# Tile loads issued one step ahead, and one slot's x and scale moved from GpSimd and ScalarE to VectorE, in the last stage of a Mamba and mixture-of-experts kernel

## Time and profile before

| | us |
|---|---|
| median of 3 runs | 1452.68 (1452.41 to 1453.63) |
| the profiled execution | 1451.61 |
| its span | 1449.9 |
| busy in it: PE | 1234.7 (85%) |
| DVE | 1030.2 (71%) |
| ACT | 929.2 (64%) |
| POOL | 849.5 (59%) |

### The profile page before, as it was taken

The page is one execution under the profiler, slowest core; times in us unless marked ns, Lnnn a source line. Parts: engine busy times, 40 slices in busy tenths (PEclk is TensorE's granted clock), DMA queues, the critical chain, the costliest instruction groups (busy, mean ns, idle before and its releaser), DMA issues. The chain is left out here.

```text
span 1449.9 us, 27240 instructions
## 1 busy us (share of the span) xinstructions
PE 1234.7 (85%) x8578; PEld 1076.1 (74%) x8578; DVE 1030.2 (71%) x3112; ACT 929.2 (64%) x2106; POOL 849.5 (59%) x1023
## 2 busy tenths in 40 slices
PE   2899999999999999999999999639999899898850
PEld 2777777778777777777877777529989898898850
DVE  4788889989989989998998998534433434443763
ACT  2777877887787787788778778434434444443443
POOL 0365566556656656655665665516666766662577
PEclk9899999999999999999999999859999999999975
DMA  5500010011011001000101000165677667664455
GB/s 167 178 8 23 26 41 31 24 33 38 24 32 38 24 24 40 31 24 33 38 24 31 32 18 17 50 181 153 172 170 164 163 167 179 155 157 107 160 168 167
DMA packets 112934, 119.90 MB, mean 83 GB/s; under 512 B 19888, under 2 KB 99056, under 8 KB 112880
## 3 DMA queue, kind: packets, MB, share of 16 engines
q1 hardware_dynamic: 97744, 94.58, 20.7%
q0 software_dynamic: 14336, 23.08, 8.3%
q10 hardware_dynamic: 800, 1.57, 0.3%
HBM read 70.63 MB, written 48.56 MB: 82 GB/s over the span
## 5 line engine op out<-in xcount | busy, mean ns | idle before, releaser
L1025 POOL TENSOR_TENSOR mamba_arena<-mamba_arena 128x512 f32<-128x512 f32 (+2 forms) x384 | 383.4, 1009 | 299.2 <-DVE mamba_arena L804 201.8
L454 PE MATMUL bank<-identity,mamba_arena 128*128 128x128 f32 x704 | 112.6, 280 | 52.8 <-DVE mamba_arena L913 27.4
L804 DVE TENSOR_TENSOR mamba_arena<-bank,mamba_arena 128x512 f32<-128x512 f32 (+1 forms) x224 | 136.4, 610 | 13.3 <-PE bank L498 7.6
L454 PEld LDWEIGHTS bank<-identity,mamba_arena 128*128 128x128 f32 x704 | 85.1, 146 | 79.9 <-issue 27.3
L1370 PE MATMUL bank<-xt_hi,wsgu_hi 128*128 128x256 f32 x384 | 116.3, 303 | 26.8 <-DVE xt_lo L1753 13.8
L1370 PE MATMUL bank<-xt_lo,wsgu_hi 128*128 128x256 f32 x384 | 111.9, 291 | 0.0
L1370 PE MATMUL bank<-xt_hi,wsgu_lo 128*128 128x256 f32 x384 | 111.8, 291 | 0.0
L662 ACT ACTIVATE mamba_arena<-bank 128x512 f32<-128x512 f32 x192 | 100.2, 539 | 9.0 <-PE bank L454 6.4
L1370 PEld LDWEIGHTS bank<-xt_hi,wsgu_hi 128*128 128x128 f32 x384 | 77.0, 201 | 28.7 <-DVE xt_lo L1753 15.0
L804 DVE TENSOR_TENSOR mamba_arena<-mamba_arena 128x512 f32<-128x512 f32 (+1 forms) x128 | 54.7, 427 | 48.9 <-ACT mamba_arena L662 46.7
L666 ACT ACTIVATE mamba_arena<-x_all,mamba_arena 128x256 f32 (+1 forms) x128 | 69.9, 595 | 20.8 <-DVE mamba_arena L850 15.5
(11 more groups left out here) (365 smaller groups left out, 4475.8 us busy)
## 6 DMA issues: line engine op xcount, KB each, us to landing
experts_arena<-in_egu SPq DMA_DIRECT2D x64, 256.0 KB, 3.4
routed_sum<-zeros SPq DMA_DIRECT2D x1, 8320.0 KB, 27.0
x_all<-in_x SPq DMA_DIRECT2D x32, 256.0 KB, 2.7
token_table<-mamba_arena SPq DMA_DIRECT2D x64, 128.0 KB, 1.7
normed_transposed<-mamba_arena SPq DMA_DIRECT2D x32, 256.0 KB, 2.0
experts_arena<-normed_transposed SPq DMA_DIRECT2D x32, 256.0 KB, 3.4
experts_arena<-in_edown SPq DMA_DIRECT2D x64, 128.0 KB, 3.0
experts_arena<-routed_sum SPq DMA_DIRECT2D x32, 256.0 KB, 3.1
```

Of the source, the lines that this page charges most:

```text
L454: return nc.tensor.transpose(out, in_, identity[:, :])
L804: return nc.vector.tensor_tensor(out, a, b, op)
L1025: return nc.gpsimd.tensor_tensor(out, a, b, op)
```

## The change

Two edits.

SP issues tiles 1 to 4 (not 1 to 3) before its wait for the last routed addition. In turn n it issues tile n + 5 (not n + 4), and no longer at the head of the turn: behind the loads of slots 1 and 3 and before the load of slot 0. The wait ahead of each load still asks that the tile two before it has been split.

Slot 2 was scaled and shifted by ACT (`f_sum * scale + shift`) and added to x by POOL. Now DVE computes `x = f_sum * scale + x` with one scalar_tensor_tensor for each sequence, right behind the shifts of its turn, and ACT adds the shift to x in place with the same two activations as before in number, size and place, now without a scale. ACT waits for DVE's two instructions. POOL's addition of slot 2 (128x512) is gone, and with it POOL's wait.

```diff
@@ SP
-                for t in range(1, LEAD + 1):
+                for t in range(1, LEAD + 2):
                     eng.wait_ge(m_xt_split, t + 7)
                     load_tile(t)
                 eng.wait_ge(added11, 256)
...
                 for n in range(9):
                     if n < 7:
-                        if n + LEAD + 1 < 8:
-                            eng.wait_ge(m_xt_split, n + LEAD + 8)
-                            load_tile(n + LEAD + 1)
                         eng.wait_ge(f_added1, n + 1)
                         load_sums(1, 2 * n + 2, routed_loaded1)
                         eng.wait_ge(f_added3, n + 1)
                         load_sums(3, 2 * n + 3, routed_loaded3)
+                        if n + LEAD + 2 < 8:
+                            eng.wait_ge(m_xt_split, n + LEAD + 9)
+                            load_tile(n + LEAD + 2)
                         eng.wait_ge(f_added0, n + 1)
@@ ACT
-                        for b in range(NB):
-                            last = nc.scalar.activation(f_sum[:, v, 2, b, :], f_sum[:, v, 2, b, :], ACT.Identity, bias=fshift[:, v, 2, b:b + 1], scale=frs[:, v, 2, b:b + 1])
-                        last.then_inc(f_normed2, 1)
+                        eng.wait_ge(f_scaled2, n)
+                        for b in range(NB):
+                            last = nc.scalar.activation(x_all[:, b, n + 15, :], x_all[:, b, n + 15, :], ACT.Identity, bias=fshift[:, v, 2, b:b + 1])
+                        last.then_inc(f_ready2, 1)
@@ DVE, behind lines 1842 and 1844
+                        for b in range(NB):
+                            last = nc.vector.scalar_tensor_tensor(x_all[:, b, n + 15, :], f_sum[:, u, 2, b, :], frs[:, u, 2, b:b + 1], x_all[:, b, n + 15, :], ALU.mult, ALU.add)
+                        last.then_inc(f_scaled2, 1)
@@ POOL
-                        eng.wait_ge(f_normed2, n)
-                        x_now = of_step(x_all, n + 15)
-                        nc.gpsimd.tensor_tensor(x_now, x_now, f_sum[:, u, 2], ALU.add).then_inc(f_ready2, 1)
```

More of the change, by code:

```diff
@@ L1208, in build @@
         f_shift0, f_shift123 = sem("f_shift0"), sem("f_shift123")
-        f_normed0, f_normed1, f_normed2, f_normed3 = sem("f_normed0"), sem("f_normed1"), sem("f_normed2"), sem("f_normed3")
+        f_normed0, f_normed1, f_normed3 = sem("f_normed0"), sem("f_normed1"), sem("f_normed3")
+        f_scaled2 = sem("f_scaled2")
         f_ready0, f_ready1, f_ready2, f_ready3 = sem("f_ready0"), sem("f_ready1"), sem("f_ready2"), sem("f_ready3")
```

## The result

| | median us | lowest to highest | runs |
|---|---|---|---|
| before, beside it on the same chip | 1452.41 | 1446.56 to 1454.28 | 7 |
| after | 1457.69 | 1454.98 to 1461.12 | 7 |

The ratio is 1.0042 (95% interval 1.0026 to 1.0058): slower, by 5.3 us between the medians. The profiled execution of the kernel after took 1455.97 us with a span of 1454.2 us.

What follows compares the result with a forecast made beforehand. A ring of waits through DVE and POOL's powers, no full engine, sets the pace. Loads -5.2, turns with a tile +5.5, without +6.4, last turn -0.2: +6.5 us, median 1459.2, 8-in-10 range 1452 to 1461.5.

Steps and rivals of the forecast that it cites:

- Loads: Issuing SP's tile loads earlier ends ACT's waits for them: -5.66 us, or -5.2 with 0.45 for three early splits.
- rival 3: Early splits hold POOL's powers 0.6 us each, and DVE's line 1883 is held once more: +9.3 us, chance 0.05.
- The pair: DVE's two new slot 2 instructions are each held by a POOL addition, making DVE 2.61 us later, not 0.78.
- x: DVE's delay at line 1852, slot 0's sum, caused by the two new instructions: 2.61 us.
- the prediction's formula: The whole change as 7x - 11.8 us for x above 0.97, zero at x = 1.69.
- T: The start of DVE's shift (line 1842) in a turn, from which the held instructions were timed; 1408.32 in turn 5.
- What comes back: Freed holds and filled DVE idleness leave turns with a tile 1.37 us longer, those without 2.14.
- ACT's wait: ACT's added wait for DVE's new instructions: at most 0.7 us a turn, costing nothing.
- The last turn: POOL does not add there, the new instructions run free, and POOL's line 2029 starts earlier: -0.2 us.
- The condition: DVE and POOL hold each other up when DVE reads two SBUF inputs.
- rival 1: Only one of DVE's two new instructions is held: x is 1.70, sum +0.1 us, 1452.8; chance 0.22.
- rival 2: Neither new DVE instruction is held, POOL's next addition is stretched instead: -5.6 us, 1447.1; chance 0.13.

Runs made afterwards that it cites:

- e1: The kernel before with the early tile loads and nothing else: 1445.49 us, 0.9956 of the kernel before.
- e6: The kernel after with POOL's third addition of a turn (slot 1 to x) waiting for DVE's new pair: 1452.12 us in one run.
- e7: The kernel after with DVE's new pair, ACT's slot 2 activations and slot 2's store put later, POOL's additions waiting for DVE's shifts: 1440.83 us, 0.9915 of before.
- e2: The kernel after with the old tile loads, so only slot 2 is moved: 1459.34 us, 1.0050 of the kernel before.
- e3: The kernel after with DVE's new pair moved behind its two instructions of slot 0's sum: 1452.26 us, 1.0000 of the kernel before.
- e5: The kernel after with the new pair as tensor_scalar, leaving x out of slot 2 so each reads one tile: 1442.37 us in one run.
- e4: The kernel after with POOL's first addition of a turn waiting for DVE's new pair: 1445.01 us, 0.9956 of the kernel before.
- e8: The kernel before with early tile loads and POOL's additions waiting for DVE's two shifts, slot 2 unmoved: 1445.74 us, 0.9950 of before.

## Why the prediction was right

It said +6.5 us on the profiled execution, and the change did +5.3; the mechanism is the one forecast: both new instructions are held by POOL's additions, and the early loads do not make up for it. Of the 1.2 us between them the loads are 0.5, the seven turns 0.55 and the last turn 0.2. Step by step:

- **Loads.** -5.66 before the splits was forecast, and -5.7 is measured (e1), turns 1 and 2 to the hundredth. (By its rows line 1644 starts 1.15 us behind 2005, not 1.17; it changes 0.02 us.) The three early splits were put at 0.15 each and cost nothing in the profiled execution. The timeline after, at the end of turn 1:

```profile
1360.62 0.88 POOL L2027 TENSOR_TENSOR experts_arena<-experts_arena,minus_half 128x2 f32<-128x2 f32 x1
...
1360.90 0.68 DVE L1835 TENSOR_TENSOR xt_lo<-experts_arena,xt_hi 128x512 fp32r<-128x512 f32 x1
1361.47 1.09 POOL L2031 TENSOR_TENSOR x_all<-x_all,experts_arena 128x512 f32<-128x512 f32 x1
```

  The split runs its plain 0.68 us beside the power, which starts first. The power takes 0.88, and as much at the end of turn 3, which has no split beside it, so the split is not what lengthens it from the 0.73 of turn 5. The turns with a split (14.14, 14.15) are as long as turn 3 (14.13). This is not always so: of the 22 early splits that start beside this power in the eight traces with early loads, three (two in e6, one in e7) brought it to 1.53 to 1.55 us and cost 0.67 each. That is over the prediction's bound of 0.6, and it is the first half of its rival 3. What decides it was not found, and how often it happens in the other six runs of the kernel after is not known.
- **The pair.** Both are held, in the order forecast. x is 2.51 us instead of 2.61. By the prediction's formula 0.1 less in x is 0.7 us over the seven turns. The arithmetic let POOL's third addition wait for the first one's end at T + 2.43, and end at T + 3.39. In the trace that addition starts at T + 2.26, when ACT had made it ready, runs its plain 1.09 and ends at T + 3.35; the second new one starts at about T + 2.29. The other half is the held one's own part: 0.34 us behind the addition's end was forecast, and 0.28 is measured.
- **What comes back.** A turn with a tile was to grow by 1.37 and grew by 1.23 (n = 1 to 3, against e1); one without by 2.14 and grew by 2.02. (Turn 7 is not like turns 5 and 6, as the prediction had it, but 0.9 us shorter, before and after, so its growth is the same.) Slot 2's sum takes 0.67 us as forecast. Turn n = 4 grew by 1.58; in it POOL's `var + eps` of slot 0 starts late, at 1403.03, and takes 0.41 instead of 0.24. The same stands in turn 4 of e2, e3 and e5, and not in e4, e6, e7 and e8; why was not found. The seven turns together: 11.35 us against e1, 11.90 forecast.
- **ACT's wait.** It was to be 0.7 at most and to cost nothing: 0.5 us, in the turns without a tile, with nobody behind it late.
- **The last turn.** -0.38 instead of -0.2.
- **The condition.** The prediction tied the hold to two SBUF inputs. That is too narrow: e5's instruction reads one tile and a scale and is held to 1.19 us. It did not matter for the number, since the new pair reads two tiles from SBUF.

The sum made with measured terms: start of turn 1 -1.5, turns 1 to 7 +7.16 (91.91 - 84.75), end -0.38, together +5.3.

**The rivals.** That only one is held (rival 1) did not happen, but e3, which makes it happen, ran at its time. That the pair is not held (rival 2) did not happen; e4 shows it held nowhere and 6.6 us under before, near the rival's -5.6, though by another order on POOL. What separated the forecast from rival 1 was whether the second of the pair starts ahead of POOL's third addition. It was behind by 0.03 us (its own record starts at 1409.27, the addition at 1409.24), and in e5, ahead by 0.10, it was free: the forecast was right here by a thin margin.

**What the prediction did not see.** Its price for slot 2 is right only with the early loads beside it, and it did not say so. With them slot 2 costs 11.0 us (+5.3 against e1's -5.7), with the old loads 6.2 (e2), and its two instructions in DVE's idle time gain 4.9 (e7 against e8). The Trainium skill's GPSIMD Engine Reference (Engine selection) advises VectorE for elementwise additions, which stood behind rival 2: the traces disagree with it where POOL adds beside (e2) and agree where it doesn't (e7).

**Open.** Turn n = 4's extra 0.33 us, when an early split stretches POOL's power, and why the start of the stage moves by up to 8 us between executions of the same code, were not followed. That a held instruction depends on the moment it starts is shown by e3 to e6; how the chip arbitrates was not measured by itself.

## What to carry to other kernels

When work goes from POOL to DVE, look up in the timeline what POOL does at the place where it lands: an instruction on DVE that costs 0.39 us alone cost 1.25 in its chain beside POOL's additions, and a place at which DVE waits anyway costs nothing. A wait that keeps the slower engine's additions off a short, critical instruction can be worth more than it delays (e4, e7). And two edits in one ring are to be tried apart and together: what one takes away (a late tile) can be what kept the other cheap.

## What the runs showed of the hardware

- A 128x256 multiply-add on DVE with SBUF inputs takes 0.48 us alone and 1.32 to 1.35 beside POOL's 128x512 additions of 1.09 us; one of 128x6 elements takes 0.17 and 1.05. The held one ends shortly behind the addition that it started behind: 0.02 us the small one, 0.28 the large one.
- An instruction that reads one tile and a scalar is held too: 1.19 us against 0.35 (e5). The pair with an input in PSUM (0.86) is not, nor are the statistics that read SBUF: two take 0.75 beside POOL's addition in e4 and 0.73 with POOL idle in the kernel after.
- Beside POOL's additions the one that starts first wins, and the line is narrow: in the kernel after DVE starts 0.03 us behind POOL and loses, in e8 its line 1883 (1407.87, 0.68 us) starts 0.05 ahead of POOL's addition at 1407.92 and wins. POOL then pays 0.1 to 0.5 us (1.19 in e5, 1.57 in e8, instead of 1.09).
- With POOL's power of 128x2 elements the start does not decide alone: in e6 it starts 0.28 us ahead of DVE's 128x512 subtraction and takes 1.55 us, one turn earlier 0.29 ahead of it and takes 0.88; the subtraction takes 0.68 to 0.69 in both.
- PE's granted clock was 0.57 over 4 us at the first products of the stage in the kernel before, mostly at the lower of its levels of 1.2 and 2.4 GHz, and 1.00 in the kernel after, behind the same 2.17 us of idleness. Of the ten traces six are of the first kind and four of the second, and it cost 1.5 us over 48 products.
